# Attention with a quantised linear layer: another order inside a unit's preparation, and the maxima turned in the middle of a block

## The reference

```python
xn = layernorm(x)
# attention: 16 heads of 16, 8 key/value heads (each serves 2 heads)
energy = q @ k.T - slope[h] * abs(i - j)          # slope[h] = 2 ** -(h + 1)
att = softmax(energy / sqrt(16)) @ v
# linear: x rounded to int8 by its row's largest, integer product, scaled back
x_q = clip(round(xn / x_scale), -128, 127)
out = x + (att @ Wo.T + bo) + (x_q @ weight_q.T * x_scale * weight_scale + bias)
```

## Time and profile before

| | |
|---|---|
| median of three runs | 1669.74 us |
| lowest, highest | 1667.75, 1669.87 us |
| the profiled execution | 1668.61 us, its span 1666.8 us |
| TensorE (PE) busy | 97% of the span |
| VectorE (DVE) busy | 86% |
| ScalarE (ACT) busy | 75% |
| GpSimd (POOL) busy | 52% |

### The profile page before, as it was taken

How to read it: one execution, slowest core, us unless ns; L and a number is a source line. 1 busy time by engine, 2 the same in 40 slices (tenths; PEclk the granted TensorE clock), 3 DMA queues, 4 the chain that set the end, 5 groups by cost and what they waited for, 6 DMA issues and landing times.

```text
span 1666.8 us, 53397 instructions
## 1 busy us (share of the span) xinstructions
PE 1611.9 (97%) x22208; PEld 761.2 (46%) x22208; DVE 1431.3 (86%) x1723; ACT 1243.4 (75%) x2489; POOL 873.4 (52%) x1401
## 2 busy tenths in 40 slices
PE   6699999999999999999999999999999999999997
PEld 5234444444444444444444444444444444444433
DVE  6799999888888888888888888888888888999981
ACT  3258777877877877877877877877777777888884
POOL 5326555655655655655655655655655654433331
PEclk9689999999999999999999999999999999999999
DMA  5302112122222222222222222222222212211112
GB/s 139 84 24 56 46 53 57 52 63 66 54 64 64 57 63 63 57 63 62 57 63 63 60 61 63 62 58 62 62 59 63 60 54 59 56 49 45 46 32 74
DMA packets 152590, 99.81 MB, mean 60 GB/s; under 512 B 90684, under 2 KB 131900, under 8 KB 152348
## 3 DMA queue, kind: packets, MB, share of 16 engines
q1 hardware_dynamic: 152348, 96.40, 21.2%
HBM read 60.16 MB, written 35.65 MB: 57 GB/s over the span
## 4 chain that ended last, share of the span: by engine, by line
PE 90%; ACT 3%; DVE 2%; DMA 1%; POOL 1%; issue 1%; SPq 1%; POOLq 0%; DVEq 0%; ACTq 0%
PE ps_ring L985 27%; PE ps_pv L1040 26%; PE ps_row L985 26%; PE ps_ring L1059 5%; PE ps_ring L1077 3%; DVE row_max L712 2%; PE ps_ring L1062 1%; ACT lin L880 1%; ACT proj L886 1%; DMA parts_dram<-parts 1%; PE ps_ring L1071 1%; ACT probs L862 1%; DMA bias<-bias_lin 0%; SPq L352 0%; POOL parts L488 0%
## 5 line engine op out<-in xcount | busy, mean ns | idle before, releaser
L712 DVE TENSOR_REDUCE row_max<-ps_row 128x1 f32<-128x1024 f32 x1024 | 1208.9, 1218 | 161.4 <-PE ps_row L985 160.6
L862 ACT ACTIVATE probs<-ps_ring 128x512 f32<-128x512 f32 x2048 | 1113.7, 600 | 215.8 <-PE ps_ring L985 170.8
L985 PE MATMUL ps_ring<-q,k 122*32 122x512 bf16 x8192 | 733.9, 381 | 13.0 <-ACT proj L886 7.9
L529 POOL TENSOR_TENSOR probs<-probs,near 128x256 f32<-128x256 f32 x512 | 378.2, 739 | 605.7 <-ACT probs L862 546.1
L985 PE MATMUL ps_row<-k,q 120*32 120x512 bf16 x8192 | 632.1, 384 | 10.7 <-DVE row_max L712 9.4
L1040 PE MATMUL ps_pv<-probs,v_unit 128*32 128x512 f32 x4096 | 529.7, 592 | 0.6 <-POOL probs L529 0.6
L985 PEld LDWEIGHTS ps_ring<-q,k 122*32 122x32 bf16 x8192 | 221.7, 95 | 378.3 <-issue 121.5
L985 PEld LDWEIGHTS ps_row<-k,q 120*32 120x32 bf16 x8192 | 220.3, 97 | 343.2 <-issue 162.8
L1040 PEld LDWEIGHTS ps_pv<-probs,v_unit 128*32 128x32 f32 x4096 | 125.3, 111 | 100.2 <-POOL probs L529 1.9
L868 ACT ACTIVATE v_all<-ps_ring 128x128 f32<-128x128 f32 x53 | 14.7, 277 | 95.5 <-PE ps_ring L1062 95.5
L1059 PEld LDWEIGHTS ps_ring<-xn_t,wqk 128*128 128x128 f32 x636 | 75.0, 191 | 22.5 <-issue 22.1
(11 more groups left out here) (78 smaller groups left out, 815.0 us busy)
## 6 DMA issues: line engine op xcount, KB each, us to landing
parts_dram<-parts SPq DMA_DIRECT2D x64, 288.0 KB, 3.0
q<-parts_dram SPq DMA_DIRECT2D x128, 96.0 KB
q<-parts_dram SPq DMA_DIRECT2D x128, 64.0 KB
att_dram<-att_unit SPq DMA_DIRECT2D x128, 64.0 KB
att_t<-att_dram SPq DMA_DIRECT2D x56, 128.0 KB, 2.3
out<-out_tile SPq DMA_DIRECT2D x55, 128.0 KB, 2.2
base<-x SPq DMA_DIRECT2D x51, 128.0 KB, 2.5
k<-parts_dram SPq DMA_DIRECT2D x64, 96.0 KB
```

What stands on the lines that cost most here:

```text
L529: pool.tensor_tensor(here, here, near[:, u % KV_HEADS, :].rearrange("p (e n) -> p e n", e=GROUP), ALU.mult).then_inc(weighted, 1)
L712: dve.tensor_reduce(row_max[:, par, e, qb:qb + 1], ps_row[qb % 2][:, :], AX_X, ALU.max, negate=True).then_inc(row_max_found, 1)
L862: act.activation(probs[:, c % PBUFS, e, h * HALF:(h + 1) * HALF], ring_bank(u, c, e, h), ACT.Exp, scale=SCALE).then_inc(ring_freed, 1)
L985: mm = pe.matmul(to[at, :], weights[:, at], moving, start=start, stop=stop)
```

## The change

In TensorE's, ScalarE's and the ring's order the preparation becomes "outputs", "turns", "qkv" instead of "qkv", "outputs", "turns". Since the turns now write `xn_t` and `xq_t` while qkv still has to read the older `xn_t`, both get two buffers, chosen by the tile's parity. "maxima" moves from behind block 5 to between the third half of block 5 and that block's `pv_block`; on ScalarE it stands before the last exponential of the block. The diff without the two-buffer indexing of the opening's functions:

```diff
@@ -101,10 +101,10 @@
         for c in range(BLOCKS):
             items = [(u, c, e, h) for e in range(GROUP) for h in range(2)]
             if c == 1:
-                items += [(u, "qkv")] * f["made"] + [(u, "outputs")] * (f["made"] or f["proj"])
-                items += [(u, "turns")] * f["turns"]
+                items += [(u, "outputs")] * (f["made"] or f["proj"])
+                items += [(u, "turns")] * f["turns"] + [(u, "qkv")] * f["made"]
             if c == 5 and not f["last"]:
-                items.append((u, "maxima"))
+                items.insert(3, (u, "maxima"))
             for item in items:
                 places[item] = len(places)
     return places
@@ -167,8 +167,8 @@
         xinv = sb("xinv", [P, SCALES, 1])
         xround = sb("xround", [P, EMBED])
         xq = sb("xq", [P, 2, EMBED], BF16)
-        xn_t = sb("xn_t", [P, EC, P])
-        xq_t = sb("xq_t", [P, EC, P], BF16)
+        xn_t = sb("xn_t", [P, 2, EC, P])
+        xq_t = sb("xq_t", [P, 2, EC, P], BF16)
         rest = sb("rest", [P, 2, QK_CHUNKS * P])
         parts = sb("parts", [P, 2, PARTS, QK_CHUNKS * P], BF16)
         qk = sb("qk", [P, 2, QK_CHUNKS * P])
@@ -808,8 +808,8 @@
         def _(act):
             def keep_xn_t(t, bank):
                 act.wait_ge(xn_turned, t + 1)
-                wait(act, qkv_made, t)
-                act.activation(xn_t[:, :, :].rearrange("p c n -> p (c n)"), bank[:, 0:EMBED],
+                wait(act, qkv_made, t - 1)
+                act.activation(xn_t[:, t % 2, :, :].rearrange("p c n -> p (c n)"), bank[:, 0:EMBED],
                                ACT.Copy).then_inc(xn_t_ready, 1)
 
             def keep_qkv(t, par, bank):
@@ -887,11 +887,11 @@
                                    ACT.Copy).then_inc(ring_freed, 1)
 
             def keep_turns(u):
-                bank = ring_bank(u, "turns")
+                t, bank = u + PREP_AHEAD, ring_bank(u, "turns")
                 wait_filled(act, u, "turns")
-                act.activation(xn_t[:, :, :].rearrange("p c n -> p (c n)"), bank[:, 0:EMBED],
+                act.activation(xn_t[:, t % 2, :, :].rearrange("p c n -> p (c n)"), bank[:, 0:EMBED],
                                ACT.Copy).then_inc(xn_t_ready, 1)
-                act.activation(xq_t[:, :, :].rearrange("p c n -> p (c n)"), xq_turn(bank),
+                act.activation(xq_t[:, t % 2, :, :].rearrange("p c n -> p (c n)"), xq_turn(bank),
                                ACT.Copy).then_inc(ring_freed, 1)
 
             def keep_maxima(u):
@@ -905,16 +905,16 @@
                 for c in range(BLOCKS):
                     for e in range(GROUP):
                         for h in range(2):
+                            if (c, e, h) == (5, 1, 1) and not f["last"]:
+                                keep_maxima(u)
                             exps(u, c, e, h)
                     if c == 1:
-                        if f["made"]:
-                            keep_qkv_whole(u)
                         if f["made"] or f["proj"]:
                             keep_outputs(u, f)
                         if f["turns"]:
                             keep_turns(u)
-                    if c == 5 and not f["last"]:
-                        keep_maxima(u)
+                        if f["made"]:
+                            keep_qkv_whole(u)
 
             act.wait_ge(qkv_made, PREP_AHEAD)
             act.wait_ge(lin_made, PREP_AHEAD)
@@ -1057,18 +1057,19 @@
                 for m in range(QK_CHUNKS):
                     for c in range(EC):
                         pe.matmul(bank[:, m * P:(m + 1) * P], wqk[:, c, m * P:(m + 1) * P],
-                                  xn_t[:, c, :], start=(c == 0), stop=(c == EC - 1))
+                                  xn_t[:, t % 2, c, :], start=(c == 0), stop=(c == EC - 1))
                 for c in range(EC):
-                    mm = pe.matmul(bank[:, QK_CHUNKS * P:], xn_t[:, c, :], wv[:, c, :],
+                    mm = pe.matmul(bank[:, QK_CHUNKS * P:], xn_t[:, t % 2, c, :], wv[:, c, :],
                                    start=(c == 0), stop=(c == EC - 1))
                 mm.then_inc(ring_filled, 1)
 
             def outputs(u, f):
                 bank = take_bank(u, "outputs")
                 if f["made"]:
+                    t = u + PREP_AHEAD - 1
                     wait_freed(pe, u - 1, "turns")
                     for c in range(EC):
-                        mm = pe.matmul(bank[:, 0:EMBED], xq_t[:, c, :], w8[:, c, :],
+                        mm = pe.matmul(bank[:, 0:EMBED], xq_t[:, t % 2, c, :], w8[:, c, :],
                                        start=(c == 0), stop=(c == EC - 1))
                 if f["proj"]:
                     done = u - OUT_BEHIND
@@ -1099,6 +1100,8 @@
                     col_half(u, c, 0, 1)
                     ahead_row_block(u, f, 2 * c)
                     col_half(u, c, 1, 0)
+                    if c == 5 and not f["last"]:
+                        turn_max(u + 1, take_bank(u, "maxima")).then_inc(ring_filled, 1)
                     if c >= 2:
                         pv_block(u, u % 2, c - 2)
                     elif f["prev"]:
@@ -1106,14 +1109,12 @@
                     col_half(u, c, 1, 1)
                     ahead_row_block(u, f, 2 * c + 1)
                     if c == 1:
-                        if f["made"]:
-                            qkv_whole(u)
                         if f["made"] or f["proj"]:
                             outputs(u, f)
                         if f["turns"]:
                             turns(u)
-                    if c == 5 and not f["last"]:
-                        turn_max(u + 1, take_bank(u, "maxima")).then_inc(ring_filled, 1)
+                        if f["made"]:
+                            qkv_whole(u)
 
             run_units(unit)
             for c in (BLOCKS - 2, BLOCKS - 1):
```

More of the change, by code:

```diff
@@ L830, in keep_xq_t @@
                 act.wait_ge(xq_turned, t + 1)
-                wait(act, lin_made, t)
-                act.activation(xq_t[:, :, :].rearrange("p c n -> p (c n)"),
+                wait(act, lin_made, t - 1)
+                act.activation(xq_t[:, t % 2, :, :].rearrange("p c n -> p (c n)"),
                                bank.bitcast(BF16)[:, 0:EMBED], ACT.Copy).then_inc(xq_t_ready, 1)
@@ L953, in make_lin @@
                 for c in range(EC):
-                    mm = pe.matmul(bank[:, 0:EMBED], xq_t[:, c, :], w8[:, c, :], start=(c == 0),
+                    mm = pe.matmul(bank[:, 0:EMBED], xq_t[:, t % 2, c, :], w8[:, c, :], start=(c == 0),
                                    stop=(c == EC - 1))
```

## The result

| | before | after |
|---|---|---|
| median | 1669.26 us (4 runs) | 1639.39 us (4 runs, 1638.80 to 1640.63) |
| ratio | | 0.9823, 95% interval 0.9806 to 0.9840 |
| profiled execution, its span | 1668.61, 1666.8 us | 1640.63, 1638.8 us |

The change takes 29.9 us off, where 25.0 were forecast. The time lies inside the range (1637 to 1653 us), at the edge of the likeliest case (1639 to 1649).

A forecast was written before the change was run, and what follows sets the result against it. TensorE's chain, with stops behind the preparation and at the maxima, was taken as the bound. Gains of 14.0 + 2.9 + 8.1 = 25.0 us took 1668.6 to 1643.6, adjusted to 1644.2 us; range 1637 to 1653.

The forecast's parts named there:

- The bound and the two stops: TensorE's order bounds the kernel; it loses 0.36 us behind the preparation and 0.25 us at the maxima.
- term of 0.31 us per full unit: Row strips behind the preparation start at 816.49 instead of 816.80; 45 x 0.31 = 14.0 us gained.
- 0 to 0.1: Entering the full array with bf16 instead of f32 weights may give back this many us; 0 was taken.
- The 0.05 for the turned `xq` before an f32 load: Preparation: short `xq` products cannot cover the following f32 load; bounds 0 and 0.10 us, 0.05 taken.
- The room of 0.06 at qkv's bank: Block 2's third half can use the bank at 816.86 and comes to it at 816.92, so no wait.
- Maxima: Turn inside block 5: product 0.12 us late instead of 0.25 lost; 62 x 0.13 = 8.1 us gained.
- The 0.07 of waiting: In block 5 the turn starts 0.07 us after its slot, its bank being held by the first half's exponential.
- Rival B: The maxima's turn drains the array, so only the preparation gains: 1652.2 us, at worst 1653.5; chance 0.11.
- Who is moved past what: SyncE's `att_t` load, needed 1.9 us earlier, has slack; GpSimd's idle 2.52 us absorbs 1.46; VectorE is free.
- the slower rival: GpSimd's split of the maxima comes late and stops TensorE at the turn: 1685.7 us if at 826.0; chance 0.03.
- A: The forecast itself, both places gaining as computed: 1644.2 us, own range 1639 to 1649; chance 0.72.
- D: Better at both places: no uncovered load, cheaper full-array entry, a turn costing 0.08: 1636.4 us; chance 0.07.

The follow-up runs named there:

- prep_only: Changed kernel with the maxima back behind block 5, so the new order of the preparation alone: 1647.58 us, ratio 0.9873.
- max_only: Kernel before the change with only the maxima moved into block 5: 1659.47 us, ratio 0.9945.
- xq_first: Changed kernel with the maxima's turn behind block 5's `ps_pv` product and the turned `xq` made first, ahead of `lin`: 1633.15 us, ratio 0.9786.
- v_twice: Changed kernel with `v_all` copied once more into a spare tile ahead of the real copy: 1644.45 us, ratio 0.9859.

## Why the prediction was right, and where it was off

*The bound and the two stops* stand. After the change no wait for `proj` is left, none for `qk` is to be seen from start to start, and prep_only and max_only show each gain alone.

*Preparation.* The term of 0.31 us per full unit was too small: 0.40 came here, alone (the rest of prep_only's 0.43 lies elsewhere in the unit) and together (of 0.54). Nearly all of the difference is the first load on the full array. The prediction gave "0 to 0.1" for the bf16 tile and took 0, "because the late row and the qkv row show the same entry". Both of those rows load f32 tiles, so they could not speak for bf16; the value was 0.09. The prediction also had the wrong name for what it read. It split 1.06 less 0.86 into 0.10 for entering and 0.10 for leaving. Leaving is 0.09 of it (0.31 from the last pass to the first strip, for 0.22), but the rest is the f32 load that nothing covers, 0.10. Entering costs 0.09 more, and they stand ahead of the first full-array product: from the last strip to it 0.31 us pass, where a strip's next product comes after 0.22. These 0.31 are the same in every kernel here, whatever the type of the tile. So the switch stayed as it was, and the load got cheaper. The 0.09 make 53 x 0.09 = 4.8 us, about the size of the whole miss (29.9 - 25.0). The 0.05 for the turned `xq` before an f32 load was a choice between 0 and 0.10 without a row; it was met (0.054 by xq_first), and that is luck. The room of 0.06 at qkv's bank was worked out and right (v_twice).

*Maxima.* 0.13 forecast; 0.14 in full units alone, 0.10 in early ones and 0.12 in late ones. The 0.07 of waiting came as worked out. That the turn would not drain the array stands as well: it is followed by the f32 product after 0.01 us (811.49, 811.50). The rule of the Trainium skill ("TensorEngine Tiling (Array Packing)", Key Properties) concerns a change of tiling mode, and here there is none. Rival B had the right question with the wrong mechanism; what a lone strip product costs is skew.

*Who is moved past what.* GpSimd and VectorE behaved as forecast (TensorE waited for VectorE's reduces 14 times in the whole execution before and 12 times after), and so did the slower rival's price once it was made real, apart from the 0.15 of the release. About SyncE the statement "there is slack" held in the changed kernel, whose trace has no wait for `att_t`, thanks to the other half of the change. With the new order alone 3.0 us are left from issue to use, enough for the usual landing of 2.3 us and not for the single ones of 4.1.

*Chances.* The time fell between A and D: D's cheaper entry with A's maxima. Giving D 0.07 was too little for two independent unknowns of which one had no row of its own type.

## What to carry to other kernels

With a small ring of banks, fill the items in such an order that the ones whose banks are needed next are emptied while the engine still works on the others, and put last the one whose copies fit into the work before its bank comes round again; then work out the room that is left, because every bit beyond it is paid in every turn of the loop. Two waits in one chain are not a sum: being late for the first may cover the second. When several orders are free, place what is short or narrow where nothing has to be loaded or realigned behind it, and judge steps of 0.05 us by the length of the loop's turn, not by the median of the whole.

## What the runs showed that I had not expected

- Entering the full array with an f32 tile of 128 columns exposes 0.10 us of its load (qkv, projection) or 0.06 (turned `xn`), with a bf16 tile 0.01.
- A product on one of four strips, behind which nothing waits, costs 0.01 us where it stands and 0.08 (0.62 for 0.54) at the next full-array product, many microseconds later; until then the strip runs behind.
- TensorE starts the turn 0.05 us after the end of ScalarE's instruction when that is what it waited for, and 0.15 after the end of GpSimd's, as the profile gives these ends.
